# The row maxima of an attention kernel go into the second score product by DMA, as two rows of its diagonal operand

## What is computed

```python
Q = split_heads(layernorm(x) @ Wq.T); K, V = split_heads(ctx @ Wk.T), split_heads(ctx @ Wv.T)
scores = einsum('bhqd,bhkd->bhqk', Q, K) / sqrt(8)
scores = where(mask == 0, -1e9, scores)
x = x + (softmax(scores) @ V, heads joined) @ Wo.T

h = layernorm(x)
probs = softmax(h @ wg.T); the two best of 8 experts, weights renormalised
y_e = (silu(h @ w1[e].T) * (h @ w3[e].T)) @ w2[e].T
x = x + sum of the two experts' y_e, weighted
```

## Time and profile before

| | |
|---|---|
| median of 3 runs | 286.79 us (285.69 to 287.94) |
| span of the profiled execution | 289.2 us |
| PE busy | 220.1 us, 76% |
| DVE busy | 214.5 us, 74% |
| ACT busy | 131.9 us, 46% |
| POOL busy | 109.8 us, 38% |
| mean granted clock of PE | 0.877 of full |

### The profile page before, as it was taken

One profiled execution on the slowest core, in us unless ns is written; L12 is line 12 of the kernel. 1 busy time (PEld: TensorE's weight loads), 2 busy tenths in 40 slices (PEclk: granted clock), 3 DMA queues, 4 the chain that ended last, 5 costly groups with the idle time before them and its releaser, 6 DMA issues.

```text
span 289.2 us, 5289 instructions
## 1 busy us (share of the span) xinstructions
PE 220.1 (76%) x1445; PEld 161.4 (56%) x1445; DVE 214.5 (74%) x619; ACT 131.9 (46%) x291; POOL 109.8 (38%) x120
## 2 busy tenths in 40 slices
PE   0787779998989988887667674688787789997620
PEld 0663456666757665665336542477566668886410
DVE  4779966688759867895977786568895568775596
ACT  5777127554665448342145546243334435453300
POOL 4310350121403070105486556104556565555530
PEclk9996579999999999979756799589899999999855
DMA  6954411353033302331602110421342232211807
GB/s 216 318 233 118 131 35 28 92 125 86 9 98 96 94 0 67 87 100 47 207 9 67 46 39 29 99 47 30 77 79 76 82 84 73 80 52 26 236 5 217
DMA packets 38108, 26.33 MB, mean 91 GB/s; under 512 B 4748, under 2 KB 35726, under 8 KB 37696
## 3 DMA queue, kind: packets, MB, share of 16 engines
q1 hardware_dynamic: 34848, 19.76, 25.5%
q0 software_dynamic: 2656, 5.40, 6.1%
q10 hardware_dynamic: 576, 0.83, 0.9%
HBM read 12.32 MB, written 6.31 MB: 64 GB/s over the span
## 4 chain that ended last, share of the span: by engine, by line
PE 42%; DVE 30%; issue 10%; SPq 8%; DMA 4%; ACT 2%; POOL 1%; another core or an unknown queue 1%; DVEq 0%; ACTq 0%; POOLq 0%
SPq L427 8%; PE bank L528 8%; DVE m_neg L1411 6%; PE bank L759 4%; PE bank L760 3%; PE bank L733 3%; PE bank L652 3%; DMA bd<-st 3%; PE bank L746 3%; PE bank L736 3%; PE bank L693 2%; PE bank L676 2%; PE bank L734 2%; PE bank L679 2%; PE bank L534 2%
## 5 line engine op out<-in xcount | busy, mean ns | idle before, releaser
L1411 DVE TENSOR_REDUCE m_neg<-bank 128x4 f32<-128x512 f32 x64 | 43.5, 684 | 15.4 <-PE bank L693 15.0
L1048 POOL DMA_INDIRECT ys<-big x39 | 38.1, 976 | 40.0 <-DVE big L1447 19.2
L923 ACT ACTIVATE big<-bank 128x512 f32<-128x512 f32 x64 | 37.4, 597 | 20.9 <-PE bank L679 20.0
L797 ACT ACTIVATE st<-bank 128x128 fp32r<-128x128 f32 (+1 forms) x78 | 22.6, 330 | 31.6 <-PE bank L746 16.1
L1004 POOL DMA_INDIRECT xg<-rows,rows_i x24 | 24.6, 1027 | 31.8 <-DVE rows_i L1218 11.6
L693 PE MATMUL bank<-bd,st 128*128 128x512 f32 x64 | 31.1, 509 | 4.7 <-DMA bd<-st 3.8
L676 PE MATMUL bank<-m_bd,ones_b 128*128 128x512 f32 x64 | 31.3, 489 | 2.1 <-ACT big L923 1.9
L759 PE MATMUL bank<-bd,st 128*128 x78 | 24.3, 332 | 9.8 <-DVE big L1447 6.2
L1355 DVE SCALAR_TENSOR_TENSOR st<-st_hi,cst,bank 128x512 fp32r<-128x512 f32 x32 | 23.3, 747 | 11.3 <-ACT st_hi L797 9.0
L1026 POOL TENSOR_TENSOR m_bd<-mT,cst 128x512 fp32r<-128x512 f32 x16 | 17.3, 1110 | 30.1 <-DVE mT L1334 30.0
L679 PE MATMUL bank<-bd,st 128*128 128x512 f32 x64 | 27.1, 423 | 0.0
(11 more groups left out here) (174 smaller groups left out, 514.0 us busy)
## 6 DMA issues: line engine op xcount, KB each, us to landing
bd<-st SPq DMA_DIRECT2D x126, 64.0 KB, 2.0
big<-xg SPq DMA_DIRECT2D x39, 64.5 KB
raw<-in_L_ffn_w SPq DMA_DIRECT2D x2, 1024.0 KB, 9.3
raw<-ys SPq DMA_DIRECT2D x6, 256.0 KB
x_all<-in_x SPq DMA_DIRECT2D x4, 256.0 KB, 4.5
rows<-in_mask_BxS_if POOLq DMA_DIRECT2D x4, 256.0 KB, 5.2
ctx_all<-in_L_ffn_w SPq DMA_DIRECT2D x1, 1024.0 KB
ctx_all<-in_ctx SPq DMA_DIRECT2D x3, 256.0 KB, 5.2
```

Of the source, the lines that this page charges most:

```text
L923: nc.scalar.activation(prob[n % 2][:, NJ * g:NJ * (g + 1), :].rearrange("p h q -> p (h q)"), s2[k % 2][:, :], ACT.Exp, scale=SCALE).then_i ...
L1048: pool.indirect_dma_start(ys, bass.IndirectOffsetOnAxis(xt[n % XR][:, D:RW].bitcast(I32), 0), y_sb[n % YR], None, bounds_check=PAIRS - 1, ...
L1411: nc.vector.tensor_reduce(m_neg[:, H * (b - 1) + NJ * g:H * (b - 1) + NJ * (g + 1)], s1[k % s1_ring(u)][:, :].rearrange("p (j q) -> p j q" ...
```

## The change

The key stacks get ones in rows 26 and 27 of the first block (a constant that ACT adds as a bias), and the query diagonal gets the two parts of a batch's maxima in its rows 26 and 27, over all 16 heads. So the score product adds them itself, and L676, `m_bd`, its POOL instructions and `ones_b` are gone. The diagonals' DMAs copy only the 26 rows in use of each block. The two rows of a batch are written by two DMAs on POOL's queue, each from 16 partitions of `mT` to one partition of the diagonal (`maxima_row`). At the start of a stage POOL issues those of the stage's first three batches; those of its fourth batch, which share a slot with the first and wait for the first's second pass, stand after `inverse_deviation`, `mask_context` and `load_mask`, and in the last stage ahead of the scatters of quartets 1 and 2.

```diff
-    c[:, C_CK] = np.where((r >= 8) & (r < 16), -1.0, 0.0)
+    c[:, C_ONE_K] = (p == MAX) | (p == MAX + 1)
+    c[:, C_CK] = np.where((r >= 8) & (r < 16), -1.0, 0.0) + c[:, C_ONE_K]
...
+        def maxima_in(engine, n):
+
+            engine.wait_ge(mrow_ready[n % 3], 32 * (n // 3 + 1))
...
-                    rows = slice(R * j, R * (j + 1))
+                    rows = slice(R * j, R * j + USED)
...
                             if g == 0:
                                 diagonal_in(pe, 0, n)
+                                maxima_in(pe, n)
...
-                            if b == 0:
-                                pe.wait_ge(mbd_ready, NG * (u - 1) + g + 1)
-                            nc.tensor.matmul(s2[k % 2][:, :], ones_b[:, b, :],
-                                             m_bd[:, NJ * g:NJ * (g + 1), :].rearrange("p h q -> p (h q)"),
-                                             start=True, stop=False)
                             nc.tensor.matmul(s2[k % 2][:, :], st[:, (u - 1) % 2, 1, g, b * S:(b + 1) * S],
                                              bd_slot(0, n)[:, g, :, :].rearrange("p j q -> p (j q)"),
-                                             start=False, stop=True).then_inc(s2_full, 1)
+                                             start=True, stop=True).then_inc(s2_full, 1)
...
-                            i = copy(st_hi[:, n % SH, :], src)
-                        else:
-                            i = nc.scalar.activation(st_hi[:, n % SH, :], src, ACT.Identity, bias=cst[:, C_ONE:C_ONE + 1])
-                        i.then_inc(sthi_ready, 1)
+                        one = C_ONE_K if is_k else C_ONE
+                        nc.scalar.activation(st_hi[:, n % SH, :], src, ACT.Identity, bias=cst[:, one:one + 1]).then_inc(sthi_ready, 1)
...
+            def maxima_row(n):
+
+                if n >= 3:
+                    pool.wait_ge(s2_full, NG * (n - 2))
+                else:
+                    pool.wait_ge(bd_cleared, 6)
+                for a in range(2):
+                    pool.dma_start(bd[MAX + a:MAX + a + 1, 3 + n % 3, :].rearrange("p (m q) -> p m q", q=P).bitcast(F32),
+                                   mT[QB * H * a + H * (n % QB):QB * H * a + H * (n % QB + 1), :].bitcast(F32)).then_inc(mrow_ready[n % 3], 16)
...
             for u in range(NQ + 1):
                 if u:
-
                     taken(pool, ("MT", u - 1))
-                    if u >= 2:
-                        pool.wait_ge(s2_full, NG * QB * (u - 1))
-                    for g in range(NG):
-                        nc.gpsimd.tensor_tensor(m_bd[:, NJ * g:NJ * (g + 1), :], mT[:, :].unsqueeze(1).to_broadcast([P, NJ, P]),
-                                                cst[:, C_HEAD + NJ * g:C_HEAD + NJ * (g + 1)].unsqueeze(2).to_broadcast([P, NJ, P]),
-                                                ALU.mult).then_inc(mbd_ready, 1)
+                    for n in range(QB * (u - 1), QB * (u - 1) + 3):
+                        maxima_row(n)
                 if u + 1 < NQ:
                     inverse_deviation(u + 1)
                     mask_context(u + 1)
...
                 if u + 1 == NQ:
                     inverse_deviation(NQ)
                     inverse_deviation(NQ + 1)
+                if u == NQ:
+                    inverse_deviation(NQ + 2)
+                if u:
+                    maxima_row(QB * u - 1)
+                if u + 1 == NQ:
                     send_quartet(0)
-            inverse_deviation(NQ + 2)
             send_quartet(1)
             send_quartet(2)
...
-                        dve.wait_ge(mbd_ready, NG * (u - 1))
+                        for n in range(QB * (u - 1) - 3, QB * (u - 1)):
+                            maxima_in(dve, n)
                     nc.vector.tensor_copy(mT[:, :], work_bank(("MT", u - 1))[:, 0:P]).then_inc(into_sbuf(("MT", u - 1)), 1)
```

More of the change, by code:

```diff
@@ L47 @@
 R = 32
+USED = 26
+MAX = USED
 QB = 4
@@ L75, in split_constant @@
     return float(hi), float(np.float32(np.float32(v) - hi))
-C_ID, C_CQ, C_CK, C_ONE, C_HEAD, C_BATCH, C_LOW, C_BIAS = 0, 128, 129, 130, 132, 148, 152, 216
-C_TRI, C_ALL, C_BASE, C_FULL, C_UPTO, C_IDS, C_STEP, C_TILE = 344, 472, 600, 608, 632, 888, 888 + 2 * B, 904 + 2 * B
+C_ID, C_CQ, C_CK, C_ONE, C_ONE_K, C_LOW, C_BIAS = 0, 128, 129, 130, 131, 132, 196
+C_TRI, C_ALL, C_BASE, C_FULL, C_UPTO, C_IDS, C_STEP, C_TILE = 324, 452, 580, 588, 612, 868, 868 + 2 * B, 884 + 2 * B
 C_N = C_TILE + NT
@@ L218, in program @@
         bias_w = sb("bias_w", [P, P], F32R)
-        ones_b = sb("ones_b", [P, QB, P], F32R)
         stats = sb("stats", [P, QB, 6])
@@ L236, in program @@
         m_hl = sb("m_hl", [P, 2, QB * H])
-        mT = sb("mT", [P, P])
-        m_bd = sb("m_bd", [P, H, P], F32R)
+        mT = sb("mT", [P, P], F32R)
         unused = sb("unused", [P, 1])
@@ L350, in program @@
         first_half = sem("first_half")
-        mbd_ready = sem("mbd_ready")
+        mrow_ready = [sem(f"mrow_ready{k}") for k in range(3)]
         s2_full, prob_ready = sem("s2_full"), sem("prob_ready")
@@ L669, in _ @@
                                 diagonal_in(pe, 0, n)
+                                maxima_in(pe, n)
                             if k >= 2:
                                 pe.wait_ge(prob_ready, k - 1)
-                            if k == 0:
-                                pe.wait_ge(setup_ready, 3)
-                            if b == 0:
-                                pe.wait_ge(mbd_ready, NG * (u - 1) + g + 1)
-                            nc.tensor.matmul(s2[k % 2][:, :], ones_b[:, b, :],
-                                             m_bd[:, NJ * g:NJ * (g + 1), :].rearrange("p h q -> p (h q)"),
-                                             start=True, stop=False)
                             nc.tensor.matmul(s2[k % 2][:, :], st[:, (u - 1) % 2, 1, g, b * S:(b + 1) * S],
                                              bd_slot(0, n)[:, g, :, :].rearrange("p j q -> p (j q)"),
-                                             start=False, stop=True).then_inc(s2_full, 1)
+                                             start=True, stop=True).then_inc(s2_full, 1)
                         if u < NQ and b >= 1:
@@ L890, in _ @@
                         src = work_bank(("st", u, k))[:, :]
-                        if is_k:
-                            i = copy(st_hi[:, n % SH, :], src)
-                        else:
-                            i = nc.scalar.activation(st_hi[:, n % SH, :], src, ACT.Identity, bias=cst[:, C_ONE:C_ONE + 1])
-                        i.then_inc(sthi_ready, 1)
+                        one = C_ONE_K if is_k else C_ONE
+                        nc.scalar.activation(st_hi[:, n % SH, :], src, ACT.Identity, bias=cst[:, one:one + 1]).then_inc(sthi_ready, 1)
                 if u == NQ:
@@ L1141, in _ @@
             nc.vector.tensor_copy(bias_w[:, :], cst[:, C_BIAS:C_BIAS + P]).then_inc(setup_ready, 1)
-            def ones_b_columns():
-                nc.vector.tensor_copy(ones_b[:, :, :], cst[:, C_BATCH:C_BATCH + QB].unsqueeze(2).to_broadcast([P, QB, P])
-                                      ).then_inc(setup_ready, 1)
             def context_rest(u):
@@ L1325, in _ @@
             split_tokens(0)
-            ones_b_columns()
             for u in range(NQ + 1):
```

## The result

The changed kernel takes 306.0 us (median of 4 runs, 303.88 to 310.36) beside 287.4 us for the kernel before on the same chip: 1.061 times as long, 95% interval 1.053 to 1.070, or 17.6 us. Some executions of a kernel are slow, 1.5% or more above its fastest; medians here are over all runs, while each ratio, and the us counted from it, goes by the others alone. The forecast was 296.8 us, with a range of 290 to 304. Slower was right. The size was not: 306.0 lies above the high end, and the loss is 7.6 us more than the +10.0 forecast.

A forecast was written before the change was run, and what follows sets the result against it. PE was taken to set the pace in b = 1 and 2, POOL's scatter chain the expert part's start. 4.1 + 2.6 + 1.8 - 0.9 + 2.4 = +10.0 us on 286.79 gave 296.8, range 290 to 304.

The forecast's parts named there:

- diagonals of 26 rows: Diagonal copies on SP's queue: landing and issue taken as unchanged, worth 0, bounds -1 and +1 us for the kernel.
- Late rows: Row 3 of a stage, issued late on POOL, stops PE at tick (3, 0): 4.1 us in stage 1, 2.6 in stage 2.
- 4.1 + 2.6 + 1.8: Losses for row 3 in stages 1 and 2, plus half clock behind those stops (1.2 us in stage 1, 0.6 in stage 2).
- The scatters: Stage 4: row 15 ahead of quartet 1 delays the scatter chain and the first expert tile by 2.4 us, bounds 1 and 4.
- The start of stage 4: First row lands at 149.0, but PE has 1.7 us of room there, so it costs nothing.
- The removed products: L676 removed 64 times: 0.5 us gained in each of stages 1 and 2, 0.9 in stage 3.
- POOL's part: POOL's L1026, 16 times 1.1 us, removed: worth nothing, except that six DMA issues take its place in POOL's queue.
- The rival of the clock in b = 0: PE idles in b = 0 of stages 1 to 3, the clock falls, steps grow 1.6 us each: 301.6 us, 15%.

The follow-up runs named there:

- experiment 5: Batch 15's row moved behind four scatters of quartet 1: on the changed kernel with 32-row copies 297.4 us; second kernel, also with early fourth rows, 290.4 us.
- experiment 8: Kernel with 32-row copies, early fourth rows and batch 15's row moved, plus dummy products (287.8 us), an earlier stage 4 start (288.1 us), or both (286.6 us).
- the filler: Dummy second-score products in batch 0 of stages 1 to 3, added to the kernel with 32-row copies, early fourth rows and batch 15's row moved: 287.8 us.
- experiment 6: Kernel before without L676, m_bd and ones_b, and without maxima rows, so maxima aren't subtracted: 286.6 us beside 291.0, ratio 0.982.
- experiment 1: Changed kernel with 32 rows a copy again, save in block 0 of the query diagonals: 301.0 us, ratio 1.047 to the kernel before.
- experiment 2: Kernel before with only the diagonals' copies cut from 32 to 26 rows a block: 299.7 us, ratio 1.048.

## Why the prediction was wrong

*The step that failed: diagonals of 26 rows.* The prediction wrote "I take landing and issue as unchanged", with bounds of -1 and +1 us "for the kernel". The issue went from 601 to 827 ns, and in the changed kernel that is worth 4.2 us (about 3.6 either way), alone 13.6. With 32-row copies the change would have cost 13.4 us: 3.4 above the forecast, and inside its range. It named the right alternative ("a slower issue would cost as much") and then priced a slower issue by one transfer a stage. An issue's cost counts once for each of the 126 on its queue, so the bound for a 10% slower issue was 126 x 0.06 = 7.6 us of SP's time, on a queue for whose diagonals PE already waited 3.8 us. The rule of the Trainium skill that it cited gave 26 rows 13 engines for 16; the prediction asked it only for the landing.

*Late rows: mechanism and places right, price too low.* "4.1 + 2.6 + 1.8" with the clock is 8.5; with 32-row copies they are worth 11.1 (interval about 3 either way), with 26-row copies 5.1. The stop lengths were within 0.2 us of the high ends named, and the granted clock was 0.50 behind both. One step of it doesn't add up: the mask load, issued at 60.23 and 5.2 us in landing, lands at 65.4 and not at "about 65.0", which would have made the term 4.5 instead of 4.1.

*The scatters: "2.4"* against some 3, inside its bounds of 1 and 4. Quartets 1 and 2 took 23.9 us from first to last scatter, 25.2 forecast.

*The start of stage 4: "1.7 us have room. Nothing"* failed. The first row was to land at 149.0, and in experiment 5's kernel L674 indeed starts at 148.85, but there was no room. POOL also came to the first row later than the forecast's 0.6 us after `mT`: 2.5 us after it in that kernel and 3.4 in the changed one, since the eighth scatter of quartet 0 stood ahead. ACT's exponentials of this tick stand ahead of ACT's part of the expert weights, DVE waits for that (2.77 us in the same trace), and DVE makes the tokens of the fill behind it. In the kernel before DVE was late at this place for another reason that left with `m_bd`: its instruction on `spread` took 1.34 us beside POOL's L1026, and takes 0.22 without it. So the room was read from a trace in which the removed work was part of what made it. The start is worth about 2 us by the runs of experiment 8, with an interval nearly as wide, and 0.9 by its traces.

*The removed products: "- 0.9"*, and 0.5 us in each of stages 1 and 2 inside the terms of the late rows: 1.9 in all. They are worth 5.1 us with nothing in their place; what the filler gave (experiment 8) suggests that the clock took some 2 more. Stage by stage, as in the table above, the trace of experiment 6 is shorter by 1.4, 0.1, 0.7 and 1.7 us in stages 1 to 4 and by 1.2 in the experts. The steps b = 0 to 2 of stages 1 and 2, where the prediction looked for most of it, gain nothing: 13.0 and 12.7 us against 12.4 and 12.3, since the step after b = 0 is 1.3 and 1.1 us longer. Stage 1 gains at its front, where PE runs its stack products at a clock of 0.50 from 41 to 43 us in the kernel before and at 1.00 in this trace, which may be chance of one execution. POOL's part, put at nothing, has about 1.1 us of DVE's time in stage 4 in it.

*The rival of the clock in b = 0*, given 15% at 301.6, did happen in the changed kernel: stages 1 to 3 each have a half-clock stretch behind b = 0, and the step after it took 6.6 us in stage 1. It was priced at 1.6 us a step; in experiment 6 the steps are 1.1 to 1.3 us longer. (The prediction called the clock whole in the 8th to the 18th slice of the kernel before; the 18th shows 7 tenths.) The window, as above:

```profile
51.90:58.50 6.60, 4.86 (x40) 3.30 (x41) 2.07 (x5) 2.17 (x4) 0.00 (x0) 0.74 0.28 57
```

It may hold a part of the 4.2 us that went with the copies' size in the changed kernel, since experiment 1's trace has a whole clock in all three of these steps. It doesn't explain the copies' price: experiment 2 has no such stretch and loses 13.6 us, and experiment 5's second kernel has all three and loses 1.1. What stays open: between that kernel (+1.1) and the bound of experiment 6 (-5.1) lie 6.2 us, of which stage 4 explains about 2: from `mT` to the first tile its trace takes 38.7 us in the one and 36.4 in the other. The two profiled executions differ by only 0.5 us in span, so the remainder is not resolved by their traces.

## What to carry over

An edit that shrinks a transfer needs the price of its issue, times the number of issues on that queue, before it is put at nothing; keep the row count one that was measured. When two late arrivals stand near each other, fix both or neither is worth its price. And room read from the old trace is room only if the removed work didn't make it.

## What the runs showed of the hardware

- On SP's queue a copy of 26 rows x 2 KB took 827 ns to issue and one of 32 rows 601; in the small kernel 30, 28, 26, 24 and 20 rows took 714 to 786 ns (medians), 8 rows 635, and 32, 31, 16 rows and 1 row 574 to 592. The last of four copies of 31 rows landed about 10 us after its issue.
- The same sizes on POOL's queue differed by 6% and the other way: 2.15 us for four of 32 rows, 2.02 for four of 26.
- Two DMAs of 8 KB from 16 partitions to one took 487 ns each on POOL's queue and 1.7 us to land at the median, less than the 0.62 (the mask load) and 2.2 (a 64 KB copy) that the forecast took.
- A DVE instruction on 128 x 64 elements took 1.34 us beside POOL's spreading of the maxima (1.58 in experiment 2) and 0.22 us without it.
- With one product a tick in place of two in a step that another wait ends, a half-clock stretch followed in 17 of 27 stages, against 1 of 12; where it came, the step behind was 1.2 to 1.7 us longer, with the granted clock at 0.71 and 0.76 of full.
